# A third of the stack pieces issued from ScalarE instead of SyncE, in an attention block with split-precision scores

## The chip, the cores and the metric

One core of a Trainium2 chip runs the whole kernel. The metric is the device time of one execution in microseconds (us). Engines are TensorE (PE; PEld is its weight load), VectorE (DVE), ScalarE (ACT), GpSimd (POOL) and SyncE (SP, which issues transfers only; SPq and ACTq are the transfer queues of SyncE and ScalarE).

## The reference

For each of 16 graphs of 512 nodes with 512 features:

```
h = relu(layernorm(x))                      # no affine part
q, k, v = h @ Wq + bq, h @ Wk + bk, h @ Wv + bv   # 16 heads of 32
scores = q @ k^T / sqrt(32), -inf where adj == 0
out = x + softmax(scores) @ v @ Wo + bo
```

All inputs are float32 (adj is int32), and so is the output.

## The kernel before

**Precision.** A matmul of the fast 32-bit type loses bits, so operands are held in two parts, hi + lo, and a product of two such operands is taken as three: hi·hi, hi·lo, lo·hi. For the projections these are three matmuls each. For the scores (a head is only 32 deep) the three products are stacked along the contraction: `q_stack` and `k_stack` hold 96 rows for each group g and head j, three bands of 32 rows, so that one matmul of 96 rows forms a score tile. One operand's stack has the order hi, hi, lo and the other's hi, lo, hi. A stack thus needs two copies of its high part, called "hi0" and "hi1", and one of its low part, "lo". Rows 96 and 97 carry the softmax's row constants (`c_rows`), which ScalarE's queue copies in (`load_c`, L492).

**A stack's way.** TensorE projects 128 columns (4 heads) of q or k into PSUM; ScalarE evicts the high part with its bias (L570), VectorE the low part (L754), both to a scratch tile named by `part_of` (y_tile, oT, part, v_sb). Then `load_stack` (its transfer is L283) copies 32 rows x 512 columns (64 KB) for each of three pieces and four heads: 12 transfers a stack, 8 stacks a graph, 96 a graph. It first waits until the scores of the graph before that read this group of the stack are done (`scores2`), and until the evictions are done (`qk_hi_done`, `qk_lo_done`). Each transfer adds 16 to the semaphore of its kind, `stack_in["q"]` or `["k"]`; a stack is complete at 192 times its running number.

**Order.** Everything is written out slot by slot. A step k has 64 slots u. In each slot TensorE does one score tile of the first pass (L914, graph k from slot 35 on, graph k-1 before) and one of the second pass (L926, from slot 60), and three or four projection matmuls (L857); 16 groups of value products (L944) stand in the slots of `PV_AT`, and the turns of h (L871, slots 1, 5, 10, 13) and of c (L875, slots 8, 24, 40, 56) between them. The first pass gives the row maxima and sums: VectorE adds the mask and takes the minimum (L688), ScalarE takes the exponential with its sum (L530, with a read-out instruction ACTIVATION_READ_ACCUMULATOR). The second pass recomputes the scores transposed with the row constant; ScalarE takes the exponential into `probs` (L586) and VectorE or GpSimd masks it (L702, L705, L444). Score banks of the first pass rotate over three, of the second over two.

ScalarE's order in slot u: L530 of slot u-1; at 16, 31, 47 and 63 the high part of O (L550); at u%4 == 0 the eviction of a projection (L570, L578); L586 of slot u; at 9, 25, 41 and 57 the two c_rows transfers (L492); the eviction of a turned h (L596).

Tile T of `TILES` is projected in slots 4T to 4T+3 and evicted in slot 4T+4. q and k tiles are evicted in slots 20, 24, 32, 36, 44, 48, 56 and 0 of the next step. SyncE loads the first six stacks a slot later (21, 25, 33, 37, 45, 49), q3 at 59, and k3 in the next step, a piece each at slots 8, 10 and 12. The first pass reads group 0 from slot 35, group 1 from 51, groups 2 and 3 from slots 3 and 19 of the next step. Between these SyncE also issues the loads of x, adj and the residual, the stores, and at slots 49 and 58 the four transposes each that turn the mask (L324). In step 0 ScalarE already issues some pieces, those of q2 and k2's first high copy one per slot behind L530 (slots 37 to 44).

Of the kernel before, what the change touches and what calls it, by code (L numbers as in the profile page):

```python
# [44 lines left out]
QK_ORDER = [x for x in TILES if x[0] in "qk"]  # L45
# [18 lines left out]
def attention_block(nc, x, adj, Wq, bq, Wk, bk, Wv, bv, Wo, bo, out):  # L64
# [9 lines left out]
    with ExitStack() as ctx:  # L74
# [60 lines left out]
        stack_in = {"q": sem("q_stack_in"), "k": sem("k_stack_in")}  # L135
# [81 lines left out]
        def tile_at(k, T):  # L217

            if k == 0:
                return QKV_TILES[T - 2] + (0,) if 2 <= T < 14 else None  # L220
            kind, n = TILES[T]
            b = k - 2 if kind == "o" else k
            return (kind, n, b) if have(b) and (kind != "o" or b != LAST) else None
# [4 lines left out]
        def have(b):  # L228
            return 0 <= b < B

        def due(count):
            return max(count, 0)
# [31 lines left out]
        def load_stack(queue, b, i, pieces=("hi0", "lo", "hi1"), heads=range(GROUP)):  # L264

            if not have(b):
                return
            kind, g = QK_ORDER[i]
            stack = q_stack if kind == "q" else k_stack
            lo_row = 64 if kind == "q" else 32  # L270
            hi_rows = [r for r in (0, 32, 64) if r != lo_row]

            queue.wait_ge(scores2, due(64 * (b - 1) + 16 * (g + 1)))
            for piece in pieces:

                if piece == "lo":
                    queue.wait_ge(qk_lo_done, due(8 * b + i + 1))
                    row, part = lo_row, part_of(b, i)[1]
                else:
                    queue.wait_ge(qk_hi_done, due(8 * b + i + 1))  # L280
                    row, part = hi_rows[int(piece[2])], part_of(b, i)[0]
                for j in heads:
                    queue.dma_start(stack[row:row + 32, g, j, :].bitcast(F32),  # L283
                                    part[32 * j:32 * j + 32, :].bitcast(F32)).then_inc(stack_loaded(b, kind, g)[0], 16)
# [11 lines left out]
        @block.sync  # L296
        def _(sp):

            def load_x(b, t):
                if have(b):  # L300
                    row = 4 * b + t

                    sp.wait_ge(h_turned, due(4 * (b - 1) + t + 1))
                    sp.dma_start(x_view(b, t), x_rows[bass.ds(row, 1)].rearrange("a p d -> (a p) d")
                                 ).then_inc(x_landed(b, t)[0], 16)

            def load_adj(b, t):
                if have(b):
                    row = 4 * b + t

                    if b > 0:
                        sp.wait_ge(bias_done, 4 * b + t)
                        sp.wait_ge(keep_done, 2 * b)
                    sp.dma_start(adj_view(b, t), adj_rows[bass.ds(row, 1)].rearrange("a p d -> (a p) d")
                                 ).then_inc(adj_landed(b, t)[0], 16)

            def turn_mask(b, half):

                if have(b):
                    sp.wait_ge(bias_done, 4 * b + 4)  # L320
                    sp.wait_ge(keep_done, due(2 * b - 1 + half))
                    sp.wait_ge(vector_masked, due(vector_before(64 * (b - 1) + 48 + 8 * half + 4)))
                    for t in range(NT):
                        sp.dma_start_transpose(turned[:, half::2, P * t:P * t + P],  # L324
                                               bias_q[:, t, 2 * P * half:2 * P * half + 2 * P]).then_inc(m_in[half], 16)

            def load_y(b, t):
                if have(b):
                    row = 4 * b + t

                    if b == LAST and t >= 2:
                        sp.wait_ge(h_turned, 4 * B)
                    else:
                        sp.wait_ge(y_out[t % 2], due(16 * (2 * b + t // 2)))
                    sp.dma_start(y_view(b, t), x_rows[bass.ds(row, 1)].rearrange("a p d -> (a p) d")
                                 ).then_inc(last_y_in[t - 2] if b == LAST and t >= 2 else y_in[t % 2], 16)

            def store_y(b, t):
                if have(b):
                    row = 4 * b + t  # L340
                    sp.wait_ge(y_done, due(4 * b + t + 1))
                    sp.dma_start(out_rows[bass.ds(row, 1)].rearrange("a p d -> (a p) d"), y_view(b, t)
                                 ).then_inc(y_out[t % 2], 16)

            def load_weight(n, w):
                if n == "o":
                    sp.wait_ge(w_lo_done["q"][0], 1)
                    sp.wait_ge(w_lo_done["q"][1], 1)
                for h in range(2):
                    sp.dma_start(w_staged[n][:, 2 * h:2 * h + 2, :], w.rearrange("(t p) d -> p t d", p=P)[:, 2 * h:2 * h + 2, :]  # L350
                                 ).then_inc(w_in[n][h], 16)

            def load_ones(g):
                sp.wait_ge(ones_set, 1)
                sp.dma_start(k_stack[STACK:STACK + 2, g].bitcast(F32), oT_hi[0:2].bitcast(F32)).then_inc(ones_done, 16)

            def step(k, parity):
                for u in range(SLOTS):
                    if u in (12, 14, 16, 18) and k > 0: load_x(k + 1, (u - 12) // 2)
                    if k == 0 and u == 27: load_weight("o", Wo)  # L360
                    if k == 0 and u == 47:
                        sp.dma_start(bo_row[:], bo.rearrange("(a d) -> a d", a=1).to_broadcast([P, D])).then_inc(bo_in, 16)
                    if u in ADJ_AT and k: load_adj(k, ADJ_AT.index(u))
                    if u < 20 and u % 4 == 1 and u >= 5: store_y(k - 2, (u - 5) // 4)
                    if u in (7, 11) and k - 2 != LAST: load_y(k - 2, (u + 1) // 4)
                    if u in ((44, 46) if k - 1 == LAST else (56, 57)):
                        if have(k):
                            sp.wait_ge(*stack_loaded(k, "q", 2))
                        load_y(k - 1, u % 2 if have(k) else (u - 44) // 2)
                    if u in (48, 50) and k - 1 == LAST: load_y(LAST, (u - 44) // 2)  # L370
                    if u == (49 if k else 35): turn_mask(k, 0)
                    if u == (58 if k else 36): turn_mask(k, 1)
                    if u in (8, 10, 12) and k > 1 and have(k - 1):
                        load_stack(sp, k - 1, 7, (("hi0",), ("lo",), ("hi1",))[(u - 8) // 2])
                    if u % 4 == 1 and u > 1:
                        done = tile_at(k, u // 4 - 1)
                        if done == ("k", 0, 0):
                            load_stack(sp, 0, 1, ("lo",))
                        elif done in (("q", 2, 0), ("k", 2, 0)):
                            load_stack(sp, 0, QK_ORDER.index(done[:2]), ("lo", "hi1"))  # L380
                        elif done and done[0] in "qk" and (done[:2] != ("q", 3) or k == 0):
                            load_stack(sp, done[2], QK_ORDER.index(done[:2]))
                    if u == 59 and k > 0 and have(k):
                        load_stack(sp, k, 6)

            for t in range(NT):
                load_x(0, t)
            load_weight("q", Wq)
            load_weight("k", Wk)
            for g in range(NT):  # L390
                load_ones(g)
            load_weight("v", Wv)
            for t in range(NT):
                load_x(1, t)
            for t in range(NT):
                load_adj(0, t)
            blocks(step, first=0)
            for s in y_out:
                sp.wait_ge(s, 16 * 2 * B)
# [81 lines left out]
        def _(act):  # L481
# [23 lines left out]
            def step(k, parity):  # L505
                for u in range(SLOTS):
# [15 lines left out]
                    if have(b):  # L522
# [10 lines left out]
                        if n % 16 == 15:  # L533
                            act.wait_ge(exp1_done, due(64 * b + n + 1))
                            act.wait_ge(c_lo_done, due(4 * b + g))
                            nc.scalar.activation(c_all[:], exp_sum[:], ACT.Ln).then_inc(ln_done, 1)
                    if k == 0 and 37 <= u < 45:
                        load_stack(act, 0, 4 + (u - 37) // 4, ("hi0",), [(u - 37) % 4])
                    if u in O_HI_AT and have(k - 1):
                        g = O_HI_AT[u]  # L540
# [434 lines left out]
```

## Time and profile before

| | |
|---|---|
| median of 3 runs | 1606.54 us (1604.37 to 1607.43) |
| the profiled execution's own time | 1606.12 us |
| its span | 1604.2 us |
| TensorE busy | 1552.0 us (97%) |
| VectorE busy | 1434.8 us (89%) |
| ScalarE busy | 1430.2 us (89%) |
| GpSimd busy | 754.6 us (47%) |
| transfers of the main queue | 179.76 MB, 41.5% of the 16 engines' span |

How to read it: times are in us unless marked ns. Busy time leaves out instructions that issue transfers. In the rows, a timeline line is start, duration, engine, line, operation, output <- input, count, and in brackets the idle time before it and what ended it. A line of waits is who waited <- for whom: us in total, times, longest. A line of a source is count: shortest/median/longest in ns. A line of stretches is from:to, length, then busy time and (count) for PE, PEld, DVE, ACT, POOL, then TensorE's granted clock, the transfer engines' share and GB/s.

### The profile page before, as it was taken

The page shows a single profiled execution, that of the slowest core. Times are in us where ns is not written, and L with a number is a line of the kernel's source. Part 1 is how long each engine was busy: PE and PEld are TensorE (multiplying, and loading weights), DVE is VectorE, ACT ScalarE, POOL GpSimd, SP SyncE. Part 2 cuts the span into 40 slices and gives each one's busy share as a digit, 9 for nine tenths or more (in the row PEclk, how much of TensorE's full clock was granted, in tenths as well). Part 3 has the DMA queues.
Part 4 walks back from the last instruction along what each step waited for, and adds up shares of the span by engine and source line. Part 5 has one row for each costly group of instructions (what it writes and reads, how often), then busy time and mean ns, then how long its engine had stood idle before and what let it go on. Part 6 is the DMA issues. An engine that isn't in the chain of part 4 may idle for free.

```text
span 1604.2 us, 27422 instructions
## 1 busy us (share of the span) xinstructions
PE 1552.0 (97%) x7489; PEld 1040.9 (65%) x7489; DVE 1434.8 (89%) x3505; ACT 1430.2 (89%) x3433; POOL 754.6 (47%) x674
## 2 busy tenths in 40 slices
PE   7899999999999999999999999999999999999987
PEld 5566666666666666666666667666666666667643
DVE  7889998998989989999998989989998998988885
ACT  4899899999989899899999989999999999989984
POOL 3245445454354445445454454445445454454442
PEclk9799999999999999999999999999999999999988
DMA  7434443534344344443444444344443444344320
GB/s 232 119 104 105 125 112 100 141 95 136 100 131 115 91 141 108 123 113 99 135 101 131 106 132 113 93 136 112 123 113 101 137 100 134 98 116 105 94 81 27
DMA packets 154064, 183.63 MB, mean 114 GB/s; under 512 B 67748, under 2 KB 69808, under 8 KB 153904
## 3 DMA queue, kind: packets, MB, share of 16 engines
q1 hardware_dynamic: 149024, 179.76, 41.5%
q10 hardware_dynamic: 4888, 2.11, 0.6%
q8 instruction: 62, 1.02, 0.3%
q14 instruction: 90, 0.74, 0.2%
HBM read 54.79 MB, written 16.78 MB: 45 GB/s over the span
## 4 chain that ended last, share of the span: by engine, by line
PE 74%; ACT 8%; SPq 7%; DVE 4%; issue 4%; DMA 2%; ACTq 1%; DVEq 0%
PE psP L857 33%; PE ps L914 14%; PE psO L944 14%; PE ps L926 12%; SPq L283 5%; ACT ps L530 4%; ACT probs L586 2%; SPq L324 2%; DVE ps L688 1%; DMA q_stack<-part_lo 1%; ACTq L492 1%; DVE probs L702 1%; PE ps L871 1%; DMA v_sb<-in_L_gnn_Wv_dram 1%; ACT hT_hi L596 1%
## 5 line engine op out<-in xcount | busy, mean ns | idle before, releaser
L444 POOL TENSOR_TENSOR probs<-probs,keep_k 128x512 int32<-128x512 int32 x438 | 574.4, 1334 | 580.7 <-ACT probs L586 579.2
L688 DVE CUSTOM_DVE_ANT_0 ps<-ps,bias_q 128x512 f32<-128x512 f32 x1024 | 706.6, 694 | 131.7 <-PE ps L914 127.3
L530 ACT ACTIVATE ps<-ps,neg_max 128x512 f32<-128x512 f32 x1024 | 687.0, 671 | 72.8 <-DVE neg_max L688 57.0
L586 ACT ACTIVATE probs<-ps 128x512 f32<-128x512 f32 x1024 | 618.0, 604 | 52.8 <-PE ps L926 25.4
L914 PE MATMUL ps<-k_stack,q_stack 96*128 96x512 f32 x1024 | 440.3, 430 | 30.5 <-ACT ps L530 26.7
L926 PE MATMUL ps<-q_stack,k_stack 98*128 98x512 f32 x1024 | 414.8, 406 | 5.6 <-ACT probs L586 4.1
L702 DVE SCALAR_TENSOR_TENSOR probs<-turned,probs 128x512 f32<-128x512 bf16 x512 | 368.0, 719 | 4.7 <-ACT probs L586 4.3
L914 PEld LDWEIGHTS ps<-k_stack,q_stack 96*128 96x128 f32 x1024 | 193.7, 189 | 222.1 <-ACT ps L530 103.9
L944 PE MATMUL psO<-probs,v_sb 128*32 128x512 f32 x2048 | 255.1, 610 | 1.7 <-ACT probs L586 1.5
L926 PEld LDWEIGHTS ps<-q_stack,k_stack 98*128 98x128 f32 x1024 | 197.0, 192 | 50.3 <-ACT probs L586 18.9
L530 ACT ACTIVATION_READ_ACCUMULATOR ps<-ps,neg_max 128x1 f32 x1024 | 216.7, 212 | 0.0
L688 DVE DVE_READ_ACCUMULATOR2_ANT neg_max<- 128x1 f32 x1024 | 143.7, 140 | 0.0
L944 PEld LDWEIGHTS psO<-probs,v_sb 128*32 128x32 f32 x2048 | 52.4, 110 | 122.9 <-issue 105.9
L857 PE MATMUL psP<-hT_hi,wq_hi 128*128 128x512 f32 x256 | 102.7, 401 | 1.3 <-ACT hT_hi L596 1.3
L857 PE MATMUL psP<-hT_lo,wq_hi 128*128 128x512 f32 x256 | 102.2, 399 | 0.0
L857 PE MATMUL psP<-wv_lo,hT_hi 128*128 128x512 f32 x256 | 101.4, 396 | 0.5 <-DVE wv_lo L666 0.5
L857 PE MATMUL psP<-wv_hi,hT_hi 128*128 128x512 f32 x256 | 101.5, 396 | 0.0
L857 PE MATMUL psP<-hT_hi,wk_hi 128*128 128x512 f32 x256 | 101.4, 396 | 0.0
L857 PE MATMUL psP<-hT_lo,wk_hi 128*128 128x512 f32 x256 | 101.2, 395 | 0.0
L857 PE MATMUL psP<-hT_hi,wq_lo 128*128 128x512 f32 x256 | 101.0, 394 | 0.0
L857 PE MATMUL psP<-wv_hi,hT_lo 128*128 128x512 f32 x256 | 100.7, 393 | 0.0
L857 PE MATMUL psP<-hT_hi,wk_lo 128*128 128x512 f32 x256 | 100.6, 393 | 0.0
(84 smaller groups left out, 1882.1 us busy)
## 6 DMA issues: line engine op xcount, KB each, us to landing
k_stack<-oT_hi SPq DMA_DIRECT2D x380, 64.0 KB, 2.0
q_stack<-y_tile SPq DMA_DIRECT2D x360, 64.0 KB, 2.0
x_tile<-in_x_dram SPq DMA_DIRECT2D x66, 256.0 KB, 3.0
y_tile<-in_x_dram SPq DMA_DIRECT2D x62, 256.0 KB, 2.9
out_dram<-y_tile SPq DMA_DIRECT2D x62, 256.0 KB, 2.0
turned<-in_adj_dram SPq DMA_DIRECT2D x61, 256.0 KB, 3.0
q_stack<-part_hi SPq DMA_DIRECT2D x240, 64.0 KB, 2.0
k_stack<-oT_lo SPq DMA_DIRECT2D x196, 64.0 KB, 2.0
```

The costliest lines, as they stand in the source:

```text
L283: queue.dma_start(stack[row:row + 32, g, j, :].bitcast(F32), part[32 * j:32 * j + 32, :].bitcast(F32)).then_inc(stack_loaded(b, kind, g)[0 ...
L324: sp.dma_start_transpose(turned[:, half::2, P * t:P * t + P], bias_q[:, t, 2 * P * half:2 * P * half + 2 * P]).then_inc(m_in[half], 16)
L444: nc.gpsimd.tensor_tensor(bits, bits, keep_k[:, kt // 2, :], ALU.mult).then_inc(gpsimd_masked, 1)
L492: act.dma_start(q_stack[STACK + part:STACK + part + 1, g, :, :].rearrange("a j (t q) -> a (j t) q", q=P).bitcast(F32), c_rows[16 * part:16 ...
L530: nc.scalar.activation(item, item, ACT.Exp, scale=-1.0, bias=neg_max[:, g % 2, col:col + 1], accum_out=exp_sum[:, col:col + 1]).then_inc(e ...
L586: nc.scalar.activation(probs[:, (SLOTS * b + n) % P_RING, :], ps2[:, n % 2, :], ACT.Exp, scale=SCALE).then_inc(exp2_done, 1)
L688: nc.vector.tensor_tensor_reduce(bank1(k, ("s", u)), bank1(k, ("s", u)), bias_q[:, qt, :], -SCALE, 3.0e38, ALU.add, ALU.min, neg_max[:, g ...
L702: nc.vector.scalar_tensor_tensor(out=tile, in0=bias_k[:, kt // 2, :], scalar=-MASKED, in1=tile, op0=ALU.add, op1=ALU.min).then_inc(vector_ ...
L857: last = nc.tensor.matmul(acc, w_l if i == 2 else w_h, m_l if i == 1 else m_h, start=(kt == 0 and i == 0), stop=(kt == NT - 1 and i == 2))
L914: nc.tensor.matmul(bank1(k, ("s", u)), q_stack[0:STACK, g, j, P * qt:P * qt + P], k_stack[0:STACK, g, j, :], start=True, stop=True).then_i ...
L926: nc.tensor.matmul(ps2[:, n % 2, :], k_stack[:, g, j, P * kt:P * kt + P], q_stack[:, g, j, :], start=True, stop=True).then_inc(scores2, 1)
L944: last = nc.tensor.matmul(psO[32 * j:32 * j + 32, :], v_sb[:, (4 * b + kt) % 6, at:at + DH], probs[:, (SLOTS * b + 4 * n + j) % P_RING, :] ...
```

## The change

From graph 1 on, the piece "hi0" of every stack is issued by ScalarE, one head per slot, behind the first exponential of the four slots after the eviction (for q3 in slots 60 to 63). SyncE issues "lo" and "hi1". Both engines first wait until the stack before, of the same kind, is complete, since both now add to one semaphore. In `load_stack`:

```
             queue.wait_ge(scores2, due(64 * (b - 1) + 16 * (g + 1)))
+            if b > 0:
+                queue.wait_ge(stack_in[kind], 192 * (4 * b + g - 4))
```

SyncE:

```
-                        load_stack(sp, k - 1, 7, (("hi0",), ("lo",), ("hi1",))[(u - 8) // 2])
+                        load_stack(sp, k - 1, 7, ((), ("lo",), ("hi1",))[(u - 8) // 2])
...
-                            load_stack(sp, done[2], QK_ORDER.index(done[:2]))
+                            load_stack(sp, done[2], QK_ORDER.index(done[:2]), ("hi0", "lo", "hi1") if k == 0 else ("lo", "hi1"))
...
-                        load_stack(sp, k, 6)
+                        load_stack(sp, k, 6, ("lo", "hi1"))
```

ScalarE, behind L530 and the row sums' logarithm:

```
+                    b, T = (k, (u - 1) // 4 - 1) if u > 4 else (k - 1, 15)
+                    done = tile_at(b, T) if u > 0 and b > 0 else None
+                    if u >= 60 and k > 0 and have(k):
+                        load_stack(act, k, 6, ("hi0",), [u - 60])
+                    if done and done[0] in "qk" and done[:2] != ("q", 3):
+                        load_stack(act, done[2], QK_ORDER.index(done[:2]), ("hi0",), [(u - 1) % 4])
```

## Rows read from the trace of the kernel before

**Rows 1.** Busy time of each engine from 100 to 1540 us.

```profile
100.00:1540.00 1440.00, 1417.51 (x6980) 962.00 (x6978) 1316.14 (x3244) 1324.67 (x3197) 700.26 (x620) 1.00 0.43 115
```

**Rows 2.** Waits of TensorE from 100 to 1540 us.

```profile
PE ps L914 <- ACT ps L530: 18.1, 44, 0.8
PE ps L914 <- DMA q_stack<-part_lo: 2.4, 8, 0.3
PE ps L914 <- DMA q_stack<-part_hi: 0.3, 1, 0.3
```

**Rows 3.** The chain by engine and line, and busy time from 244.3 to 262.0.

```profile
PE 74%; ACT 8%; SPq 7%; DVE 4%; issue 4%; DMA 2%; ACTq 1%; DVEq 0%
PE psP L857 33%; PE ps L914 14%; PE psO L944 14%; PE ps L926 12%; SPq L283 5%; ACT ps L530 4%; ACT probs L586 2%; SPq L324 2%; DVE ps L688 1%; DMA q_stack<-part_lo 1%; ACTq L492 1%; DVE probs L702 1%; PE ps L871 1%; DMA v_sb<-in_L_gnn_Wv_dram 1%; ACT hT_hi L596 1%
...
244.30:262.00 17.70, 17.07 (x85) 11.29 (x84) 15.99 (x38) 15.85 (x37) 10.46 (x10) 1.00 0.43 107
```

**Rows 4.** Weight loads of slots 51 and 3, chain at 745.03, ScalarE's read-out.

```profile
722.06 0.19 PEld L914 LDWEIGHTS ps<-k_stack,q_stack 96*128 96x128 f32 x1 [0.84 <-DMA q_stack<-y_tile]
...
745.03 1.82 DMA q_stack<-part_lo
...
746.50 0.22 ACT L530 ACTIVATION_READ_ACCUMULATOR ps<-ps,neg_max 128x1 f32 x1
...
746.83 0.19 PEld L914 LDWEIGHTS ps<-k_stack,q_stack 96*128 96x128 f32 x1 [0.70 <-DMA q_stack<-part_lo]
```

**Rows 5.** Issues of L283 (one of its forms) and L492, and L492's landing.

```profile
L283 SPq DMA_DIRECT2D q_stack<-y_tile x360: 507/590/1825, 100.2 to 1491.4; - x180
...
L492 ACTq DMA_DIRECT2D q_stack<-c_rows x128: 510/574/863, 58.8 to 1574.8; - x128
DMA to landing us min/median/max: 1.8/1.9/3.7
```

**Rows 6.** SyncE's last pieces of k0, TensorE's first matmul of slot 35.

```profile
789.36 2.49 SPq L283 DMA_DIRECT2D k_stack<-oT_hi  x4
...
794.59 0.39 PE L914 MATMUL ps<-k_stack,q_stack 96*128 96x512 f32 x1
```

**Rows 7.** ScalarE at the turn of a step, no issue between.

```profile
744.30 0.66 ACT L530 ACTIVATE ps<-ps,neg_max 128x512 f32<-128x512 f32 x1
...
744.98 0.59 ACT L586 ACTIVATE probs<-ps 128x512 f32<-128x512 f32 x1
```

**Rows 8.** ScalarE in step 0, with a piece behind L530.

```profile
38.63 0.66 ACT L530 ACTIVATE ps<-ps,neg_max 128x512 f32<-128x512 f32 x1 [0.47 <-DVE neg_max L688]
38.70 0.51 ACTq L283 DMA_DIRECT2D q_stack<-oT_hi  x1
...
39.31 0.65 ACT L530 ACTIVATE ps<-ps,neg_max 128x512 f32<-128x512 f32 x1
39.36 0.67 ACTq L283 DMA_DIRECT2D q_stack<-oT_hi  x1
...
40.13 0.69 ACT L570 ACTIVATE oT_hi<-psP,cols 128x512 fp32r<-128x512 f32 x1
```

**Rows 9.** Issues of ScalarE and SyncE at the same time.

```profile
804.49 0.53 ACTq L492 DMA_DIRECT2D q_stack<-c_rows  x1
...
804.96 0.59 SPq L283 DMA_DIRECT2D k_stack<-oT_lo  x1
...
805.05 0.79 ACTq L492 DMA_DIRECT2D q_stack<-c_rows  x1
```

**Rows 10.** The c_rows pair of slot 25, and L926 of slot 28.

```profile
781.11 0.67 ACT L530 ACTIVATE ps<-ps,neg_max 128x512 f32<-128x512 f32 x1
781.52 0.52 ACTq L492 DMA_DIRECT2D q_stack<-c_rows  x1
...
782.07 0.61 ACTq L492 DMA_DIRECT2D q_stack<-c_rows  x1
782.73 0.66 ACT L530 ACTIVATE ps<-ps,neg_max 128x512 f32<-128x512 f32 x1 [0.34 <-DVE neg_max L688]
...
784.58 0.40 PE L926 MATMUL ps<-q_stack,k_stack 98*128 98x512 f32 x1
```

## The prediction

> **What bounds the kernel now.** I read the busy shares by stretch first, then who waited for whom, then the chain of waits, and last the order of instructions on three engines in one step. From 100 to 1540 us TensorE is busy for 1417.51 of 1440 us at granted clock 1.00 [rows 1]. All that it can still win there is the remaining 22.5 us, 1.4% of the run. Its waits for other engines in that stretch are 18.1 us for the first exponential on ScalarE (44 times) and 2.4 + 0.3 us that are put down to a stack transfer [rows 2]. So the kernel is at TensorE's own pace, and ScalarE, with VectorE ahead of it, is the only partner that stops it by more than 3 us.
>
> The chain of waits says something else: SyncE's queue at L283 has 5% of the span, some 80 us, and L324 2% [rows 3]. I don't believe it. While the chain runs through SyncE from 244.3 to 262.0, TensorE is busy for 17.07 of 17.70 us [rows 3]: nobody stood still for that queue. The wait on which the chain hangs is read wrongly, too. At 746.83 TensorE loads weights for L914, "released" by a q_stack piece that was issued at 745.03 and took 1.82 us, so landed at 746.85, after the instruction that it is said to release [rows 4]. This is slot 3 of a step, where the scores of group 2 begin; they wait for q_stack's count of 192(4b-1), and this late piece belongs to group 3 and counts beyond that. What did end the wait is the exponential whose read-out ran from 746.50 to 746.72 [rows 4]. The other such pattern, 0.84 us at 722.06, is slot 51, where group 1 begins, and the piece named (from y_tile, i = 4) belongs to group 2 [rows 4]; TensorE itself was busy there.
>
> **What the change takes from SyncE.** Of the 96 pieces of 32 rows a step (8 stacks, 3 copies, 4 heads), 32 go to ScalarE. At a median of 0.590 us each [rows 5] SyncE issues 19 us less a step. Who waited for them? The tightest group is the first: k0's last four pieces are issued from 789.36 for 2.49 us; with some 2 us to land (the 1.82 us above is one) they are in at about 793.4, and the first matmul of slot 35 runs at 794.59 without a wait [rows 6]. Slack 1.2 us, and no wait to remove. The mask transposes start up to 5 us earlier, which shortens a wait on GpSimd, which is idle half the time and whose products ScalarE and TensorE don't wait for in the list of waits. Value taken for all of this: 0. Bounds: a gain of 2.7 us (every wait put down to a stack [rows 2] was real) and, as the outer end, the whole 22.5 us; a loss is excluded on SyncE's side, since its two added waits (for the stack before of the same kind, which includes ScalarE's pieces) are for transfers of 12 slots earlier.
>
> **What it adds to ScalarE.** 32 issues a step, 480 in 15 steps. In the program each stands behind the first exponential (L530) and its read-out, and ahead of whatever comes next: an eviction or the second exponential (L586). The copies that it issues belong to an eviction of its own, at least one slot older, so their waits are met. What a piece costs is the engine's spacing with and without it. Without one, L530 at 744.30 is followed by L586 at 744.98: 0.68 us [rows 7]. With one, in step 0, where exactly this edit is in place already: L530 at 38.63, issue at 38.70 for 0.51 us, next activation at 39.31: 0.68 us, nothing added. The next one took 0.67 us and the engine went on at 40.13 instead of 39.31 + 0.68 = 39.99: 0.14 us added [rows 8]. So the issue runs beside the activation that was dispatched before it, and what counts is whether it is done within some 0.6 us. An issue of 0.61 us, as the second of a c_rows pair shows [rows 10], gives 0.05 + 0.61 + 0.05 = 0.71, or 0.03 us added. L492's median is 0.574 us with a maximum of 0.863 [rows 5]. I take 0.04 us a piece; bounds 0 and 0.14 us (the third wait that a later step adds to a piece is in this bound, no row shows it alone).
>
> Do two engines that issue at once hold each other up? ScalarE's issues at 804.49 (0.53 us) and 805.05 (0.79 us) lie over SyncE's of 0.59 us at 804.96 [rows 9]: SyncE loses nothing, ScalarE 0 to 0.2 us. The Trainium skill ("Perfetto Trace Analysis", the DMA timeline under "Per-instruction lifecycle") has the descriptor generator locked for exclusive use during an issue. Were it one lock for both engines, each of the 32 pieces would wait up to another 0.59 us and the time would come out as in rival 2 or above it; these rows of overlapping issues speak against it.
>
> ScalarE is busy for 1324.67 of 1440 us [rows 1], so 480 x 0.04 = 19 us find room in 115 us of idle time; they count only where ScalarE runs without a gap and TensorE waits at the end of it. That is the cluster of slots 63 to 3 in each step (eviction of O, of k3, two turns of h), which ends in the wait at 746.83. It holds 3 pieces (slots 63, 1 and 2): 15 x 3 x 0.04 = 1.8 us. With 4 pieces at the upper bound: 15 x 4 x 0.14 = 8.4 us. The pieces of slots 21 to 28, 33 to 40 and 45 to 52 I price at 0: TensorE's own pace covers them, and if it didn't in the one other cluster (slots 49 to 52) that would again be up to 8.4 us.
>
> One place is tighter. In slot 25 ScalarE issues k0's first piece and then the c_rows pair, and the second exponential stands between them. The pair now goes out at 781.52 and 782.07; with the piece ahead (781.16 to about 781.7) L586 is dispatched some 0.2 us later and the pair with it: second issue at about 782.3. Landing at the median of 1.9 us [rows 5] is 784.2, and the matmul that needs it (L926 of slot 28) runs at 784.58 [rows 10]: 0.4 us of slack are left. The exponential behind the pair moves from 782.73 to about 783.0, and its bank is wanted a slot later. Cost 0, until landing takes over 2.3 us; the maximum in the run is 3.7 [rows 5].
>
> **Sum.** Against the profiled execution's own 1606.12 us (span 1604.2 and 1.9 around it): -0 + 1.8 = 1607.9. The median of the runs is 1606.54, 0.4 above it: 1608.3. I say 1608.
>
> The Trainium skill ("DMA: Bandwidth & Descriptors", "Issuing engines are not separate DMA queues") says that issuing from several engines saves the sequencer's issue time alone, usually small beside the transfer. By that rule the gain is SyncE's 19 us a step and nothing in the transfers; the trace agrees in so far as an issue takes 0.59 us beside some 2 us to land. A reader who takes the chain's 5% at its word would expect a third of it, 27 us, which is over the 22.5 us that TensorE can win at all.
>
> **Rivals.**
> 1. SyncE's queue was a real brake. For it: the chain, 2.7 us of named waits, the long queue from 244 to 262. Against it: TensorE's 17.07 of 17.70 us, the landing after its own release. Price: between -2.7 us and -22.5 us; with a third of the outer end, -7.5, it gives 1599. Chance 0.18 for anything over 0.2%.
> 2. ScalarE's cover is too short: the issue takes over about 0.61 us with its waits, each piece costs 0.14 us in the cluster of slots 63 to 3, and TensorE waits that much longer: +8.4 us, 1615. It decides from 3.2 / (15 x 4) = 0.053 us a piece. For it: the 0.67 us issue, and contention as at 805.05. Against it: 0.51 us at 38.70. Chance 0.22.
> 3. The c_rows pair of slot 25 comes late behind the stack pieces on ScalarE's own queue: landing of 2.8 us instead of 1.9 makes L926 wait 0.5 us in each of 15 steps: +7.5 us, with the 1.8 above 1616. For it: the maximum of 3.7 us. Against it: that pieces of both queues already share the engines, at 1.9 us. Chance 0.10.
>
> **How the numbers follow.** Forecast (1607 to 1610) 0.50, rivals as above. What this measurement can tell from no change is 0.2%, 3.2 us: faster 0.18, same 0.50, slower 0.32. The range runs from 1602, below the 2.7 us gain, to 1618, above rivals 2 and 3; it leaves the outer gain out.
>
> **What would show it.** ScalarE has 480 L283 issues more, of some 0.52 to 0.61 us, and L530 to the next activation stays near 0.68 to 0.72 us; the waits of TensorE for L530 go from 18.1 us to about 20; the list still names a stack piece at slots 3 and 51, now perhaps another. SyncE's share of the chain shrinks or moves with no change in time. Wrong would be: L926 waiting for c_rows 15 times (rival 3); issues of 0.7 us or more on ScalarE and PE waits for L530 of 25 us or more (rival 2); TensorE idle for under 18 us from 100 to 1540 (rival 1).

## The result, and the profile after

| | before | after |
|---|---|---|
| median | 1606.99 us (4 runs) | 1621.78 us (4 runs) |
| ratio, 95% interval | | 1.0093 [1.0074, 1.0112] |
| span of the profiled execution | 1604.2 us | 1618.6 us |

The change costs 15 us. The forecast was no measurable change, 1608 us, with a range up to 1618; the result lies above the range.

SyncE is out of the chain, as it would be if its queue had been the brake, and the time is longer all the same. Part 4 of the page of the changed kernel, by engine and by line (it answers to [rows 3]; all line numbers from L273 on have moved by 2 to 8: L530 is L532, L536 L538, L586 L594, L283 L285, L492 L494, L702 L710, L914 L922, L926 L934):

```profile
PE 75%; ACT 10%; DVE 6%; issue 4%; ACTq 3%; DMA 2%; SPq 0%; DVEq 0%
PE psP L865 32%; PE psO L952 15%; PE ps L922 14%; PE ps L934 12%; ACT ps L532 5%; ACT probs L594 3%; DVE ps L696 2%; ACTq L285 2%; DVE probs L710 1%; ACTq L494 1%; DMA q_stack<-c_rows 1%; PE ps L879 1%; ACT oT_hi L558 1%; DMA v_sb<-in_L_gnn_Wv_dram 1%; ACT oT_hi L578 1%
```

The stretch from 100 to 1540 us (it answers to [rows 1]) and TensorE's waits in it ([rows 2]) say little by themselves:

```profile
100.00:1540.00 1440.00, 1412.29 (x6917) 950.85 (x6917) 1309.06 (x3214) 1320.28 (x3166) 692.35 (x613) 1.00 0.44 114
```

```profile
PE ps L922 <- ACT ps L532: 23.3, 57, 1.0
PE ps L934 <- DMA q_stack<-c_rows: 2.1, 3, 1.0
PE ps L934 <- ACT probs L594: 1.0, 3, 0.6
```

TensorE is idle for 27.7 us instead of 22.5, and it does less work in the stretch (6917 matmuls instead of 6980). The rest of the loss is not shown as idle time. Of one wait at L934, for instance, the weight load shows 0.50 us and the matmul behind it none (at 805.51, below). So I looked for the place in another way. Both kernels run the same 1024 first-pass score matmuls in the same order. I took the start of each in both traces and added up, for each slot of a step, by how much the distance from the start before it is longer in the changed kernel (14 or 15 steps, so each sum is good to some 0.3 us):

```
slot   38     39     2      45     55     61     all slots
us    +3.9   +3.9   +1.9   +1.6   +1.4   +1.4    +14.4
```

At slots 38 and 39 it is 0.26 and 0.28 us in practically every step. At 2 it is spread (-0.6 to +0.7), at 45, 55 and 61 it is one to three steps, up to 1.3 us in one.

Slots 38 and 39 lead back to ScalarE in slot 35. First the kernel before, then the changed one, where the exponential of slot 34's scores, the last of its group, is followed by the logarithm of the row sums (timeline of ScalarE; the last line is TensorE's):

```profile
795.44 0.66 ACT L530 ACTIVATE ps<-ps,neg_max 128x512 f32<-128x512 f32 x1
796.02 0.19 ACT L530 ACTIVATION_READ_ACCUMULATOR ps<-ps,neg_max 128x1 f32 x1
796.25 0.21 ACT L536 ACTIVATE c_all<-exp_sum 128x16 f32<-128x16 f32 x1
796.37 0.58 ACT L586 ACTIVATE probs<-ps 128x512 f32<-128x512 f32 x1
```

```profile
801.68 0.66 ACT L532 ACTIVATE ps<-ps,neg_max 128x512 f32<-128x512 f32 x1
802.26 0.19 ACT L532 ACTIVATION_READ_ACCUMULATOR ps<-ps,neg_max 128x1 f32 x1
802.49 0.21 ACT L538 ACTIVATE c_all<-exp_sum 128x16 f32<-128x16 f32 x1
802.57 0.51 ACTq L285 DMA_DIRECT2D q_stack<-part_hi  x1
803.13 0.60 ACT L594 ACTIVATE probs<-ps 128x512 f32<-128x512 f32 x1 [0.43 <-DMA q_stack<-part_lo]
...
805.51 0.19 PEld L934 LDWEIGHTS ps<-q_stack,k_stack 98*128 98x128 f32 x1 [0.50 <-ACT probs L594]
```

The program makes the logarithm wait until the read-out of the last exponential is over (802.26 and 0.19 us; it starts at 802.49), so it can't be handed to the engine early, and nothing behind it can. The stack piece goes out at 802.57, 0.89 us behind the start of L532, where everything that could have covered it is done; only the logarithm's 0.21 us lie beside it. The second exponential starts 1.45 us after L532 instead of 0.93: 0.52 us lost, in a place where ScalarE has an eviction (L578) in the next slot. In 14 steps the median of this distance is 1.45 us in the changed kernel and 0.93 before. TensorE meets it two slots later, since the second pass has two score banks: the exponential ends at 803.73 and L934 of slot 37 starts at 803.78; the next one, late too, ends at 805.46 and L934 of slot 38 starts at 805.51. The bracket names "DMA part_lo", a transfer of SyncE's with which ScalarE has nothing to do here; it is the engine's own issue.

### The profile page after: what moved, and what is told of

The parts are those of the page before. It is cut to its first block, busy times and chain, and to the rows that moved or that the text cites. A ratio compares the mean times of both kernels' runs of the same rounds, so it can differ in the third digit from the quotient of the medians.

```text
span 1618.6 us, 27902 instructions
## 1 busy us (share of the span) xinstructions
PE 1559.0 (96%) x7489; PEld 1038.1 (64%) x7489; DVE 1440.4 (89%) x3505; ACT 1438.2 (89%) x3433; POOL 755.1 (47%) x674
## 4 chain that ended last, share of the span: by engine, by line
PE 75%; ACT 10%; DVE 6%; issue 4%; ACTq 3%; DMA 2%; SPq 0%; DVEq 0%
PE psP L865 32%; PE psO L952 15%; PE ps L922 14%; PE ps L934 12%; ACT ps L532 5%; ACT probs L594 3%; DVE ps L696 2%; ACTq L285 2%; DVE probs L710 1%; ACTq L494 1%; DMA q_stack<-c_rows 1%; PE ps L879 1%; ACT oT_hi L558 1%; DMA v_sb<-in_L_gnn_Wv_dram 1%; ACT oT_hi L578 1%
## 5 line engine op out<-in xcount | busy, mean ns | idle before, releaser
L532 ACT ACTIVATE ps<-ps,neg_max 128x512 f32<-128x512 f32 x1024 | 687.0, 671 | 62.0 <-DVE neg_max L696 43.7
L594 ACT ACTIVATE probs<-ps 128x512 f32<-128x512 f32 x1024 | 619.4, 606 | 76.2 <-PE ps L934 29.5
L922 PE MATMUL ps<-k_stack,q_stack 96*128 96x512 f32 x1024 | 440.1, 430 | 32.7 <-ACT ps L532 32.3
L934 PE MATMUL ps<-q_stack,k_stack 98*128 98x512 f32 x1024 | 417.8, 409 | 9.8 <-ACT probs L594 5.2
L710 DVE SCALAR_TENSOR_TENSOR probs<-turned,probs 128x512 f32<-128x512 bf16 x512 | 368.4, 720 | 7.0 <-ACT probs L594 6.1
L922 PEld LDWEIGHTS ps<-k_stack,q_stack 96*128 96x128 f32 x1024 | 193.7, 189 | 221.8 <-ACT ps L532 104.3
L934 PEld LDWEIGHTS ps<-q_stack,k_stack 98*128 98x128 f32 x1024 | 196.5, 192 | 68.8 <-ACT probs L594 32.7
L532 ACT ACTIVATION_READ_ACCUMULATOR ps<-ps,neg_max 128x1 f32 x1024 | 216.9, 212 | 0.0
```

The lines of the kernel that those rows point to most:

```text
L532: nc.scalar.activation(item, item, ACT.Exp, scale=-1.0, bias=neg_max[:, g % 2, col:col + 1], accum_out=exp_sum[:, col:col + 1]).then_inc(e ...
L594: nc.scalar.activation(probs[:, (SLOTS * b + n) % P_RING, :], ps2[:, n % 2, :], ACT.Exp, scale=SCALE).then_inc(exp2_done, 1)
L710: nc.vector.scalar_tensor_tensor(out=tile, in0=bias_k[:, kt // 2, :], scalar=-MASKED, in1=tile, op0=ALU.add, op1=ALU.min).then_inc(vector_ ...
L922: nc.tensor.matmul(bank1(k, ("s", u)), q_stack[0:STACK, g, j, P * qt:P * qt + P], k_stack[0:STACK, g, j, :], start=True, stop=True).then_i ...
L934: nc.tensor.matmul(ps2[:, n % 2, :], k_stack[:, g, j, P * kt:P * kt + P], q_stack[:, g, j, :], start=True, stop=True).then_inc(scores2, 1)
```

## The experiments

All ratios are to the kernel before, run on the same chip (4 runs of the changed kernel, 6 of e2 and e3, 11 or 12 of the others). A loss at a slot always means the sum of above, against the trace of the kernel before. It comes from one execution, the ratio from all. e1's profiled execution was the slowest of its twelve, 3.8 us above their median.

| | median, us | ratio [95%] |
|---|---|---|
| changed kernel | 1621.8 | 1.0093 [1.0074, 1.0112] |
| e1 pieces ahead of the logarithm | 1609.9 | 1.0024 [1.0011, 1.0038] |
| e2 one piece a step, behind the logarithm | 1614.5 | 1.0050 [1.0033, 1.0068] |
| e3 first high copy not issued | 1615.5 | 1.0051 [1.0031, 1.0071] |
| e4 = e1, q3 and k2 back with SyncE | 1607.0 | 1.0005 [0.9989, 1.0021] |
| e5 = e3, adj's load later | 1606.9 | 0.9999 [0.9987, 1.0010] |
| e6 = e2, one slot later | 1606.7 | 1.0000 [0.9987, 1.0012] |
| e7 before, logarithm later | 1605.9 | 0.9993 [0.9980, 1.0007] |
| e8 changed, logarithm later | 1609.7 | 1.0019 [1.0006, 1.0033] |
| e9 = e1, q3 back | 1609.4 | 1.0022 [1.0010, 1.0034] |
| e10 = e1, k2 back | 1606.2 | 1.0000 [0.9988, 1.0011] |
| e11 = e1, second transposes later | 1610.6 | 1.0026 [1.0013, 1.0040] |
| e12 = e1, GpSimd's second addition later | 1607.4 | 0.9997 [0.9986, 1.0009] |

**e1: the same 480 pieces, ahead of the logarithm.**

```
                                              accum_out=exp_sum[:, col:col + 1]).then_inc(exp1_done, 1)
-                        if n % 16 == 15:  ... logarithm (L538)
                     if done and done[0] in "qk" and done[:2] != ("q", 3):
                         load_stack(act, ... the piece as before)
+                    if have(b) and n % 16 == 15:  ... logarithm
```

> The changed kernel with one difference: ScalarE's stack pieces stand ahead of the row sums' logarithm (L538) instead of behind it; only slots with n % 16 == 15 (35, 51, 3) differ. Theory A (missing cover): behind the logarithm, which waits for L532's read-out, the issue begins 0.8 us later and the second exponential with it, 0.5 us a step at slot 35; with the piece ahead, TensorE's loss of 0.26 + 0.28 us at slots 38 and 39 is gone: 15 x 0.54 = 8.1 us less than the changed kernel, so about 1613.5 us, 6 to 7 us above the kernel before. Theory B (the 480 issues cost ScalarE a little each, wherever they stand): no change against the changed kernel, 1621. Theory C (issues on ScalarE are stretched by SyncE's issues and transposes): no change at slots 38 and 39 either, 1621.

The gain is 0.7% of 0.93%, some 11 us, more than the 8.1 that I had expected (1609.9 instead of 1613.5). Slots 38 and 39 lose nothing any more (0.3 us in 14 steps, together), and of the 4.4 us at slots 45, 55 and 61 under 1 us is left, though the pieces there stand as they did. ScalarE's timeline in e1:

```profile
798.15 0.66 ACT L532 ACTIVATE ps<-ps,neg_max 128x512 f32<-128x512 f32 x1
798.24 0.51 ACTq L285 DMA_DIRECT2D q_stack<-part_hi  x1
798.74 0.19 ACT L532 ACTIVATION_READ_ACCUMULATOR ps<-ps,neg_max 128x1 f32 x1
798.96 0.21 ACT L544 ACTIVATE c_all<-exp_sum 128x16 f32<-128x16 f32 x1
799.08 0.58 ACT L594 ACTIVATE probs<-ps 128x512 f32<-128x512 f32 x1
```

The issue runs beside the activation, and the second exponential is 0.93 us behind the first, as in the kernel before. Theories B and C are out for this part.

**e2 and e6: one piece a step, in slot 35 or in slot 36.**

```
+                    if u == 35 and k > 0 and have(k):          # e6: 36
+                        load_stack(act, k, 2, ("hi0",), [2])   # e6: [3]
```

with SyncE leaving out that one piece.

> The kernel before with a single piece per step moved to ScalarE: head 2 of q1's first high copy, in slot 35 behind the logarithm (15 issues in all instead of 480). Both engines have the added wait for the stack before. Theory A: this piece alone costs 0.54 us a step at slots 38 and 39: 8.1 us, 1614 to 1615. Theory B: 15 of 480 issues, under 0.5 us: 1607. Theory C: under 1 us: 1607.

> The kernel of e2 with the single piece one slot later (head 3 in slot 36, behind L532 with no logarithm between). Theory A: covered, 1605 to 1608, the same as before. If any lone piece on ScalarE costs 0.5 us in this place, 1614 as e2.

Fifteen issues in the whole run cost 8 to 9 us in slot 35 (by the interval 5 to 11) and nothing that can be measured in slot 36. This is the sharpest pair of the study. ScalarE in e6 from the logarithm of slot 35 on (here L536 is the first exponential and L542 the logarithm; the piece stands behind the L536 of slot 36, at 796.61):

```profile
796.01 0.22 ACT L542 ACTIVATE c_all<-exp_sum 128x16 f32<-128x16 f32 x1
796.14 0.58 ACT L594 ACTIVATE probs<-ps 128x512 f32<-128x512 f32 x1
796.45 0.53 ACTq L285 DMA_DIRECT2D q_stack<-part_hi  x1
796.61 0.65 ACT L536 ACTIVATE ps<-ps,neg_max 128x512 f32<-128x512 f32 x1
797.19 0.20 ACT L536 ACTIVATION_READ_ACCUMULATOR ps<-ps,neg_max 128x1 f32 x1
797.28 0.68 ACT L578 ACTIVATE oT_hi<-psP,cols 128x512 fp32r<-128x512 f32 x1
```

The issue starts 0.16 us ahead of the exponential that it stands behind in the program: that one had been handed to the engine and waited only for its turn. The next activation comes 0.67 us behind it.

**e8 and e7: the logarithm behind the second exponential**, with two buffers for the sums.

```
+                    if have(b) and n % 16 == 15:     # behind L594 (L586)
+                        nc.scalar.activation(c_all[:], exp_sum[:, g % 2, :], ACT.Ln).then_inc(ln_done, 1)
```

> The changed kernel, its 480 pieces where they are, with the logarithm moved as in e7, so that no piece stands behind a logarithm. Theory A: the 8 us of slots 38 and 39 go as in e1: 1608 to 1612. Theory B or C: 1621.

> The kernel before with the row sums' logarithm (L536) behind the second exponential of its slot instead of ahead of it, and two buffers for the sums so that the next group need not wait for it. Ahead, it holds L586 until L530's read-out is over: 0.93 us between the two activations instead of 0.66, four times a step. Theory A (what stands behind the logarithm loses its cover) gives ScalarE 0.27 us back in each; TensorE waits near these slots only around slot 3, so 0 to 4 us faster: 1602 to 1606. If the logarithm's place is of no account: 1606.

e8 is the third way to the same place: the pieces stay where they are, the logarithm goes, and 12 us of the 15 are back. e7 shows that ScalarE's four times 0.27 us in the kernel before are worth nothing that can be measured (0.9993, the interval holds 1).

**e3: a third of the pieces not issued at all.** The kernel leaves out this part of the scores from graph 1 on, and its output is off by it; so is that of e5.

```
-            return (stack_in[kind], 192 * (4 * b + g - 3)) if b else (first_stack_in[kind][g], 192)
+            return (stack_in[kind], 128 * (4 * b + g - 3)) if b else (first_stack_in[kind][g], 192)
...
-                            load_stack(sp, done[2], QK_ORDER.index(done[:2]))
+                            load_stack(sp, done[2], QK_ORDER.index(done[:2]), ("hi0", "lo", "hi1") if k == 0 else ("lo", "hi1"))
```

> The kernel before without the first high copy from graph 1 on: the 480 pieces are not issued at all, and the band of 32 rows keeps graph 0's values (this part of the scores is left out). SyncE issues 64 pieces a step instead of 96, ScalarE none. If SyncE's queue was a brake (the chain's 5%, rival 1 of the prediction), this is faster by 2.7 us or more, up to 22 us. If it wasn't, as forecast, the time stays within 0.2% of the kernel before: 1605 to 1608.

I expected no change and it is 0.5% slower, with 480 transfers fewer. 7.2 of the 9.5 us lie at slot 29, in nine of fifteen steps. SyncE's and ScalarE's queues and TensorE, first in the kernel before, then in e3, at the same place of the same step:

```profile
395.76 0.61 ACTq L492 DMA_DIRECT2D q_stack<-c_rows  x1
396.14 0.53 SPq L314 DMA_DIRECT2D turned<-in_adj_dram  x1
```

```profile
398.82 0.81 ACTq L492 DMA_DIRECT2D q_stack<-c_rows  x1
398.82 0.52 SPq L314 DMA_DIRECT2D turned<-in_adj_dram  x1
...
402.19 0.50 PE L926 MATMUL ps<-q_stack,k_stack 98*128 98x512 f32 x1 [0.70 <-DMA q_stack<-c_rows]
```

SyncE, relieved of four pieces, issues the 256 KB load of adj 0.38 us sooner against ScalarE's second c_rows transfer (8 KB), so that both set out together. TensorE waits for c_rows 11 times between 100 and 1540 us, 6.1 us in all, where before there was none. The fifteen steps of e3 part cleanly: in the nine in which the load sets out within 0.02 us of the second c_rows transfer, that one takes 2.97 to 3.67 us to land and TensorE waits at slot 28; in the six in which it sets out 0.15 to 1.08 us later, landing takes 1.9 to 2.2 us and nobody waits.

**e5: e3 with the load of adj behind one piece of k0.**

```
+                            if k > 0 and u == 25:
+                                load_stack(sp, k, 1, ("lo",), (0,))
+                                load_adj(k, 1)
+                                load_stack(sp, k, 1, ("lo",), (1, 2, 3))
+                                load_stack(sp, k, 1, ("hi1",))
```

> The kernel of e3 (no first high copy from graph 1 on, that part of the scores left out) with one order changed on SyncE: the 256 KB load of adj that stands at slot 24 is issued behind the first piece of k0 instead of ahead of it, some 1.5 to 2 us later. e3 was 9 us slower than before with 7.2 us of it at slot 29: there SyncE, being early, issues that load at 398.82, in the same moment as the second c_rows transfer (398.82), where before it came 0.4 us behind; L926 of slot 28 then waits for c_rows. If this meeting is the cause (theory D), the loss goes and with it the last doubt on SyncE's queue: 1604 to 1608, same as before. If fewer pieces on SyncE cost in some other way, it stays at 1614 to 1616.

The loss is gone (slot 29: under 1 us) and the time is that of the kernel before. This settles two things: the meeting of the two transfers was e3's loss, and a third less on SyncE's queue brings nothing that can be measured, as forecast.

**e4, e9 and e10: the last 0.24% of e1.** In e1's trace 3.0 of the 4.1 us lost between 100 and 1540 us lie at slot 2. These give q3's pieces (slots 60 to 63), k2's (49 to 52) or both back to SyncE, and ScalarE leaves them out (its side of the edit is not shown):

```
+    ("hi0", "lo", "hi1") if k == 0 or done[:2] == ("k", 2) else ("lo", "hi1")     # e4, e10
+    load_stack(sp, k, 6)                                                          # e4, e9
```

> The kernel of e1 with the pieces of k2 and q3, which are issued near SyncE's mask transposes, given back to SyncE (24 pieces a step stay with ScalarE). Theory C: the issues of 1.0 to 1.7 us on ScalarE (five in the changed kernel, those looked at beside a transpose of 2.1 us) go, and with them some 3 to 4 us of losses at slots 45, 55 and 61: 1609 to 1611. Theory A says nothing on them; if the rest of the loss is spread over all pieces (theory B) a quarter of it goes, 1 to 2 us: 1612.

> The kernel of e1 (pieces ahead of the logarithm) with q3's pieces of slots 60 to 63 given back to SyncE. e1 was 3.9 us above the kernel before, e4, which gives back q3's and k2's, 1.1 us. In e1's profile 3.0 us of the rest lie at slot 2, in e4's none. Theory E: q3's pieces put the activations of slots 62 and 63 later and this reaches TensorE at slot 2: 1606 to 1608 here, nothing lost at slot 2. Rival: it is k2's pieces beside the transposes; then this stays at 1609 to 1611.

> The kernel of e1 with k2's pieces of slots 49 to 52, which are issued beside the mask's first transposes, given back to SyncE and q3's left with ScalarE. Theory E: 1609 to 1611, as e1, with the loss at slot 2 still there. Rival (issues stretched beside transposes): 1606 to 1608.

e4 came out at 1607.0, better than both theories had it (1609 to 1612). Theory E fell: with q3's pieces away, which stand right ahead of slot 2, the ratio stays at 1.0022 (e9), and k2's, ten slots earlier, make up the difference (e10: 1.0000, slot 2 at -1.8 us against before). In e9's trace slot 2 does lose 1.4 us instead of 3.0, so q3's pieces may have a part in that place; the ratio doesn't show it. But it is not in the way of theory C either: in e1's trace 97 of ScalarE's issues overlap a transpose, and they take 0.54 us on average, as all others. What moving k2's pieces does is to leave SyncE sooner free for the second group of mask transposes (the last one is issued in slot 60 in the changed kernel and e1, in 62 before, in 61 or 62 in e10), and with them comes GpSimd's work. The changed kernel around slot 63 (GpSimd, VectorE, TensorE):

```profile
842.87 0.62 POOL L454 TENSOR_SCALAR keep_k<-turned 128x512 int32<-128x512 bf16 x1 [0.91 <-DMA turned<-bias_q]
843.57 1.28 POOL L429 TENSOR_TENSOR y_tile<-y_tile,bo_row 128x512 f32<-128x512 f32 x1
...
843.03 0.68 DVE L696 CUSTOM_DVE_ANT_0 ps<-ps,bias_q 128x512 f32<-128x512 f32 x1
843.64 0.13 DVE L696 DVE_READ_ACCUMULATOR2_ANT neg_max<- 128x1 f32 x1
843.64 1.76 DVE L710 SCALAR_TENSOR_TENSOR probs<-turned,probs 128x512 f32<-128x512 bf16 x1
845.32 0.69 DVE L696 CUSTOM_DVE_ANT_0 ps<-ps,bias_q 128x512 f32<-128x512 f32 x1
...
848.80 0.50 PE L922 MATMUL ps<-k_stack,q_stack 96*128 96x512 f32 x1 [0.80 <-ACT ps L532]
```

VectorE's mask operation, 0.68 us otherwise, starts 0.07 us after GpSimd's addition and takes 1.76 us: until the addition ends (844.85) and 0.55 us more. Three slots on, TensorE waits 0.80 us for the exponential that depends on it. The Trainium skill ("SBUF — State Buffer", "Who interferes with whom") says that a VectorE operation with two SBUF inputs and a GpSimd operation that reads SBUF share a port pair, and the second to start is blocked until the first is done. By that rule 0.07 us of difference in the start decide over 1.1 us; this row agrees.

**e11 and e12: this meeting taken away in two ways.** e11 delays the transposes by four pieces; e12 leaves SyncE and ScalarE alone and puts GpSimd's second addition from slot 63 to slot 1 of the next step:

```
-                    if u == (54 if k - 1 == LAST else 63): add_bo(k - 1, 1)
+                    if u == 54 and k - 1 == LAST: add_bo(k - 1, 1)
+                    if u == 1 and k - 2 != LAST: add_bo(k - 2, 1)
```

> The kernel of e1 with GpSimd's second addition to y_tile (L429 of slot 63) two slots later in its program, in slot 1 of the next step; SyncE and ScalarE as in e1. Theory F: the stretched VectorE operations leave slot 63 and slot 2's loss of 3.0 us goes or moves a slot or two on: 1605 to 1609. Rival (pieces on ScalarE, or SyncE's earlier transfers by themselves): 1609 to 1611.

> The kernel of e1 with SyncE's second group of mask transposes (slot 58) behind the first four pieces of q3 instead of ahead of them, 2.5 us later. In e1 and in the changed kernel these transposes end in slot 60, in the kernel before and in e10 in slots 61 and 62; with them GpSimd's keep_k and its addition to y_tile come a slot earlier, into slots 62 and 63, and VectorE's mask operations that begin in slot 63 take longer: above 0.70 us they add up to 9.3 us in e1 and 8.5 us in the changed kernel, but 1.5 us before and in e10. Theory F: this meeting on GpSimd and VectorE is the rest of the loss; with the transposes later it is gone from slot 63 and slot 2 loses nothing: 1605 to 1608. Rival (it is the number of pieces on ScalarE, 480 as in e1): 1609 to 1611.

e12 is where the kernel before is, with all 480 pieces on ScalarE. What VectorE's mask operations (L710 and L713) take above 0.70 us, added up for those that begin in slot 63, 1 and 4, in 14 steps ("-" is under 0.8):

```
us               slot 63   slot 1   slot 4   loss at slot 2 against before
before             1.5       4.1      -            -
changed kernel     8.5       -        -          +1.9
e1                 9.3       -        -          +3.0
e10                1.5       2.3      -          -1.8
e12                -         -        3.9        -2.2
e11                -         -        8.7        -1.5
e9                 6.9       -        -          +1.4
e5                 6.6       -        -          +0.5
```

The last line is a bound on this account. In e5, too, SyncE is early and the meeting takes place in slot 63, but ScalarE has no pieces, slot 2 hardly loses and the time is that of the kernel before (0.9999). So the meeting alone costs nothing that can be measured. It costs with the pieces on ScalarE, and either without the other is free: e5 has the meeting, e12 the pieces. How the two act together was not tested further.

In e11 my guess failed on the time (1610.6 instead of 1605 to 1608) and was half right on the place. Slot 63 and slot 2 are clean, but the meeting moved on with the transposes to slot 4, and slots 7 and 8 lost 4.5 us. The total stayed at 1.0026. Later is not better than earlier; what counts is beside what it falls.

No version is measurably faster than the kernel before.

## Why the prediction was wrong

1. **The term for slots 33 to 40, priced at 0, was 7.8 us.** "TensorE's own pace covers them" was argued from the average slot, and the cover of 0.6 us from [rows 7] and [rows 8], where an exponential or an eviction comes next. Of the 32 places of a piece in a step, three (slots 3, 35, 51) stand behind the logarithm, with no cover at all. I had the program's order in front of me and its cost was in the kernel before as well: 0.93 us from L530 to L586 instead of 0.66. It shows in slot 35, where ScalarE has an eviction in the next slot (in e2's trace slots 38 and 39 again lose 4.1 and 4.0 us). In slots 51 and 3 ScalarE loses as much: the median distance from L530 to L586 goes from 0.93 to 1.46 us and from 1.01 to 1.48 us. But no loss of TensorE follows there; why, was not tested.

2. **"A loss is excluded on SyncE's side" was wrong.** The gain of 0 was right (e5), and TensorE's busy share and the landing after its own release [rows 3, 4] had said so. But a transfer that sets out sooner meets others: the load of adj with c_rows in e3 (0.5% slower with fewer transfers), and in the changed kernel the transposes' followers on GpSimd with VectorE, and c_rows with the loads of y_tile (below). I had counted the transposes as harmless since GpSimd is idle half the time; what it does, not how much, was the question.

3. **The 1.8 us of the cluster of slots 63 to 3 came out as 1.9 us, by luck.** The cause was another. With the logarithm's place mended it was 3.0, and e12 takes it away with every piece in its place. So the issues by themselves cost nothing there; they cost together with the meeting in slot 63 (e5 beside e1).

4. **The cost of a covered issue was right, or too high.** It was taken as 0.04 us. ScalarE's median distance from L530 to the next activation goes from 0.68 to 0.70 us at slots 24 and 34 and stays at 0.66 us at slots 36 and 37. There are 480 issues more; those from part_hi show a median of 0.515 us and a maximum of 0.557, below the 0.61 from which it would count, and nine of the 480 are above it. Answer to [rows 5], from the page of line L285 of the changed kernel:

```profile
L285 ACTq DMA_DIRECT2D q_stack<-part_hi x120: 514/515/557, 117.0 to 1525.5; - x120
...
L285 SPq DMA_DIRECT2D q_stack<-part_lo x120: 507/590/1682, 119.3 to 1525.8; - x120
```

Rival 2 had the sign and, with 8.4 us, over half of the size, by the wrong mechanism: it spread a small cost over many pieces. Its sign, TensorE's waits for L530 of 25 us or more, told nothing: they came to 23.3, where I had forecast 20. Five of ScalarE's issues in this trace took 1.0 us or more, four of them beside a transpose, in slot 52 of steps 5, 6, 13 and 14. In three of these steps, 5, 13 and 14, lies the whole loss of slot 55, 1.4 us. That is the part of rival 2 that happened. The largest one holds back the second exponential, and TensorE waits for it:

```profile
1314.32 1.73 ACTq L285 DMA_DIRECT2D k_stack<-oT_hi  x1
...
1316.10 0.60 ACT L594 ACTIVATE probs<-ps 128x512 f32<-128x512 f32 x1 [0.73 <-issue]
...
1316.74 0.50 PE L934 MATMUL ps<-q_stack,k_stack 98*128 98x512 f32 x1 [0.56 <-ACT probs L594]
```

5. **Rival 3, c_rows late at slot 28,** didn't come true at that slot in the changed kernel, but it did in e3, by a mechanism that I had not named. The slack of 0.4 us was read rightly; what it was threatened by was a 256 KB load, not the stack pieces. In the changed kernel c_rows is late elsewhere: the three waits of 2.1 us in all are at slot 60 of steps 1 and 9 (0.57 and 0.44 us) and at slot 44 of step 10 (1.04 us), and these are the steps in which slots 61 and 45 lose. At slots 57 and 58 a c_rows transfer takes over 2.9 us to land in 12 of 15 steps, up to 4.9, where in the kernel before it is 2 of 15, up to 3.7. SyncE's two loads of y_tile (256 KB each) now go out just ahead of c_rows and the transposes right behind it; before, c_rows went out at 924.47 and the loads from 926.10 on. Step 9 in the changed kernel:

```profile
931.39 1.02 SPq L337 DMA_DIRECT2D y_tile<-in_x_dram  x2
932.44 1.18 ACTq L494 DMA_DIRECT2D q_stack<-c_rows  x2
933.03 3.31 SPq L326 DMA_TRANSPOSE turned<-bias_q  x2
...
937.39 0.50 PE L934 MATMUL ps<-q_stack,k_stack 98*128 98x512 f32 x1 [0.44 <-DMA q_stack<-c_rows]
```

The account of the changed kernel's 14.4 us, from its trace: 7.8 the logarithm (slots 38 and 39; e1, e2, e6, e8), 1.9 at slot 2 (the meeting of slot 63 beside the pieces; e10, e12), 1.4 at slot 55 (long issues beside the transposes), 3.0 at slots 45 and 61 (c_rows late). The first is shown by experiments that take it away and put it back, the second by experiments that take it away; the last two are read from this one trace and were not tested. By the medians the shares come out otherwise: e1 and e8, which mend nothing but the logarithm's place, win back 11 and 12 us, and e12 the other 4. The intervals, 0.19% to either side for the changed kernel and 0.14% for e1, leave room for both readings, and whether the single late steps belong to the change or differ from one execution to the next stays open: e12's trace shows 1.7 us at 45 and at 61 too, with six waits for c_rows (1.7 us), without being slower than the kernel before.

## What to carry to other kernels

In this kernel a transfer's issue was free on a computing engine only while that engine still had dispatched work to do; look at what stands right ahead of it in the program, above all at an instruction that waits for the engine's own last result, and try it there with a single piece. Where a queue is relieved, ask what it now does sooner and beside what. And read a chain of waits against the busy share of the engine that is said to have waited: here 5% of the span hung on a queue for which nobody waited.

## What the runs showed of the hardware

ScalarE takes instructions ahead of their turn: a transfer behind an exponential was issued 0.16 us before that exponential began (e6), and 0.09 us after it in e1. Two engines mostly issue at once without loss: of ScalarE's 606 issues after 80 us in e1, the 420 that overlap one of SyncE's took 0.54 us on average and the other 186 took 0.53. Single ones are longer: in the changed kernel four beside a transpose took 1.0 to 1.7 us. An 8 KB transfer that set out within 0.02 us of a 256 KB load took 2.97 to 3.67 us to land instead of 1.9 and held TensorE up by 0.3 to 1.1 us (nine steps of e3); 0.15 us of lead were enough to avoid it. VectorE's operation with two SBUF inputs went from 0.68 to 1.76 us beside a GpSimd addition of 1.28 us.
